# x[dst] stored turned: the first layer without its turn and its bias addition, and 391 gathers in place of 392

## The reference

```
row, col = src, dst                               # 50000 each, sorted by dst
h = (x @ W).reshape(N, 4, 32)
alpha = leaky_relu(s_src[row] + s_dst[col], 0.2)  # s_*: h times a vector, per head
ex = exp(alpha - m[row])                          # m: segment max over row, at least 0
alpha_n = ex / denom[row]
out = segment_sum(alpha_n * h[col], col) + bias
x = layernorm(x + out)
```

## Time and profile before

| what | us |
|---|---|
| median of 3 runs | 5133.67 |
| lowest and highest | 5132.33, 5134.39 |
| profiled execution | 5133.19 |
| its span | 5131.1 |

### The profile page before, as it was taken

The page is one execution under the profiler, slowest core; times in us unless marked ns, Lnnn a source line. Parts: engine busy times, 40 slices in busy tenths (PEclk is TensorE's granted clock), DMA queues, the critical chain, the costliest instruction groups (busy, mean ns, idle before and its releaser), DMA issues. The chain is left out here.

```text
span 5131.1 us, 72170 instructions
## 1 busy us (share of the span) xinstructions
PE 3158.9 (62%) x15758; PEld 2416.0 (47%) x15758; DVE 3395.8 (66%) x11785; ACT 2872.1 (56%) x7156; POOL 3650.5 (71%) x3635
## 2 busy tenths in 40 slices
PE   3555555545562666256477746666988787777774
PEld 3555455533441444145466644444555465555552
DVE  6587655658887777467399973333677776666664
ACT  0014666638874888268367762333455566666663
POOL 5777777767775777478677717776777677777777
PEclk9985555569986888689688878898556598888897
DMA  3336888868882777356478858887677632222222
GB/s 72 79 80 190 250 253 255 249 124 250 251 245 67 225 226 225 111 161 200 136 202 222 221 158 246 224 226 208 194 214 210 186 74 71 73 71 71 72 72 61
DMA packets 820081, 862.65 MB, mean 168 GB/s; under 512 B 161385, under 2 KB 595150, under 8 KB 819228
## 3 DMA queue, kind: packets, MB, share of 16 engines
q1 hardware_dynamic: 703656, 673.59, 43.0%
q0 software_dynamic: 112896, 179.36, 15.8%
q10 hardware_dynamic: 3314, 7.36, 0.4%
HBM read 494.63 MB, written 370.82 MB: 169 GB/s over the span
## 5 line engine op out<-in xcount | busy, mean ns | idle before, releaser
L1929 POOL DMA_INDIRECT gs_xs<-t_t,kept_idx_b x392 | 369.9, 944 | 229.7 <-issue 118.9
L1035 POOL DMA_INDIRECT t_alpha<-gsm_raw,gsm_edge_idx x392 | 386.1, 985 | 165.8 <-issue 116.7
L2193 POOL DMA_INDIRECT mss_xs<-t_x,kept_idx_a x392 | 387.2, 988 | 144.7 <-issue 118.2
L2185 POOL DMA_INDIRECT out_dram<-mss_o,kept_scat_idx x392 | 396.1, 1011 | 119.4 <-issue 118.2
L1227 PE MATMUL gsm_hp<-kept_w,gsm_zT 128*128 128x128 f32 x1568 | 253.9, 311 | 352.3 <-ACT gsm_zT L1093 351.9
L2049 POOL DMA_INDIRECT gs_xs<-t_z,kept_idx_a x392 | 369.9, 944 | 137.5 <-issue 119.2
L1598 POOL DMA_INDIRECT att_xs<-t_t,kept_idx_a x392 | 372.0, 949 | 134.2 <-issue 118.0
L1025 POOL DMA_INDIRECT gsm_raw<-t_al,kept_idx_b x392 | 378.4, 965 | 124.4 <-issue 118.6
L536 POOL DMA_INDIRECT sort_xs<-in_x_dram,kept_src_idx x392 | 379.5, 968 | 119.5 <-issue 119.5
L534 POOL DMA_INDIRECT sort_xd<-in_x_dram,kept_dst_idx x392 | 379.4, 968 | 119.4 <-issue 119.4
L216 PE MATMUL gs_tp<-kept_ident,gs_xs 128*128 128x128 f32 x784 | 268.9, 362 | 270.4 <-DMA gs_xs<-t_t,kept_idx_b 156.6
(11 more groups left out here) (556 smaller groups left out, 11023.8 us busy)
## 6 DMA issues: line engine op xcount, KB each, us to landing
t_t<-sort_o SPq DMA_DIRECT2D x61, 858.0 KB
t_x<-gsm_o SPq DMA_DIRECT2D x196, 264.0 KB
sort_x<-in_x_dram SPq DMA_DIRECT2D x61, 832.0 KB
gsm_x<-t_t SPq DMA_DIRECT2D x196, 256.0 KB
t_z<-gsm_z SPq DMA_DIRECT2D x196, 256.0 KB
out_dram<-gsm_o SPq DMA_DIRECT2D x196, 256.0 KB, 3.0
t_t<-l_o SPq DMA_DIRECT2D x49, 528.0 KB, 3.0
att_own<-t_t SPq DMA_DIRECT2D x98, 264.0 KB
```

The costliest lines, as they stand in the source:

```text
L1035: pool.indirect_dma_start(T["alpha"], bass.IndirectOffsetOnAxis(edge_idx[:, c:c + 1], 0), raw[:, c, :], None).then_inc(scattered[u], 16)
L1929: pool.indirect_dma_start(xs[u][:, j, :], None, T["t12"], bass.IndirectOffsetOnAxis(K["idx_b"][:, c:c + 1], 0)).then_inc(gathered[u], 16)
L2185: pool.indirect_dma_start(T["out"], bass.IndirectOffsetOnAxis(K["scat_idx"][:, c:c + 1], 0), o[q % BUFS][:, j, :], None, bounds_check=N - ...
L2193: pool.indirect_dma_start(xs[q % BUFS][:, j, :], None, T["x3"], bass.IndirectOffsetOnAxis(K["idx_a"][:, c:c + 1], 0)).then_inc(gathered[q ...
```

## The change

1. The sort stage stores `xdT`, which ACT has copied from PSUM, instead of the gathered rows: a table `xdstT` of 98 x 128 rows of 512 numbers (2 KB, as before). `xdT` has four buffers. The wait for this store moves from POOL's gather to ACT's copy, and SP's store moves from slot s to slot s+1.
2. The first layer loads the turned tiles into `xT` (four buffers), multiplies them at once, and turns them back: `accumulate_turned` puts x and the turned bias (made once, at the start) into one PSUM buffer `back`. ACT copies that to `x`, POOL adds once. ACT's order in a slot becomes root (item s-3), copy (s), apply (s-3); DVE's lags fall by two. SP's load waits for the multiply and the turn back of item s-4.
3. The 392nd chunk is left out of the gathers in five stages and of the last scatter, and the waits count 16 less for the last item. `gat_softmax` is as it was.

```diff
+FILLED = -(-E // P)
+def chunks_of(q):
+    return min(4 * q + 4, FILLED) - 4 * q
+def landed(t, u, each=16):
+    if is_item(t, u, ITEMS - 1):
+        return each * (4 * t + chunks_of(ITEMS - 1))
+    return 4 * each * t + 4 * each
+def turned_rows(table, t, u, width=4):
+    rows = table[bass.ds(t * (BUFS * P * width // 4) + u * (P * width // 4), P * width // 4), :]
+    return rows.rearrange("(k p) f -> p k f", p=P)
+def as_turned_rows(tile):
+    return tile.rearrange("p (k j) i -> p k (j i)", j=4)
...
# scores_and_sort
-        xdT = [sb(f"xdT{v}", [P, 4, P]) for v in range(2)]
+        xdT = [sb(f"xdT{u}", [P, 4, P]) for u in range(BUFS)]
...
-                wait_item(pool, xd_stored, t, u, 4, 16)
                 wait_item(pool, turned, t, u, 4)
-                for j in range(4):
+                for j in range(chunks_of(q)):
...
             def copy(t, u):
                 act.wait_ge(turned[u], t + 1)
                 wait_item(act, scored, t, u, 2)
-                act.copy(xdT[u % 2][:], tpd[u % 2][:]).then_inc(copied[u], 1)
+                wait_item(act, xd_stored, t, u, 4, 16)
+                act.copy(xdT[u][:], tpd[u % 2][:]).then_inc(copied[u], 1)
...
             def store_xd(t, u):
-                sp.wait_ge(gathered[u], 128 * t + 128)
-                sp.dma_start(tile_rows(T["xdst"], t, u), as_tile_rows(xd[u][:])).then_inc(xd_stored[u], 16)
+                sp.wait_ge(copied[u], 2 * t + 1)
+                sp.dma_start(turned_rows(T["xdstT"], t, u), as_turned_rows(xdT[u][:])).then_inc(xd_stored[u], 16)
...
-            parts = [(store_o, BEFORE + 2, WIDES), (load_x, BEFORE - 2, WIDES), (store_al, 3), (store_xd, 0)]
+            parts = [(store_o, BEFORE + 2, WIDES), (load_x, BEFORE - 2, WIDES), (store_al, 3), (store_xd, 1)]
...
# first_layer
             def load(t, u):
-                wait_item(sp, summed, t, u, 4)
-                sp.dma_start(as_tile_rows(x[u][:]), tile_rows(T["xdst"], t, u, G)).then_inc(loaded[u], 16)
+                wait_item(sp, multiplied, t, u, 4)
+                wait_item(sp, turned_back, t, u, 4)
+                sp.dma_start(as_turned_rows(xT[u][:]), turned_rows(T["xdstT"], t, u, G)).then_inc(loaded[u], 16)
...
-            def shift(t, u):
-                pool.wait_ge(turned[u], t + 1)
-                pool.tensor_tensor(x[u][:], x[u][:], K["bias0"][:].unsqueeze(1).broadcast_to([P, G, D]), ALU.add).then_inc(shifted[u], 1)
...
-            pipeline(pool, (add, 3, EIGHTS), (shift, 1, EIGHTS))
+            pipeline(pool, (add, 0, EIGHTS))
...
-            def turn(t, u):
+            def multiply(t, u):
                 pe.wait_ge(loaded[u], 16 * t + 16)
-                wait_item(pe, copied, t, u, 1)
-                for j in range(G):
-                    tr = pe.transpose(tp[:, j, :], x[u][:, j, :], K["ident"][:])
-                tr.then_inc(turned[u], 1)
-
-            def multiply(t, u):
-                pe.wait_ge(copied[u], t + 1)
                 wait_item(pe, scaled, t, u, 2)
                 for j in range(G):
-                    mm = pe.matmul(hp[u % 2][:, j, :], xT[u % 2][:, j, :], K["wh"][:], start=True, stop=True)
+                    mm = pe.matmul(hp[u % 2][:, j, :], xT[u][:, j, :], K["wh"][:], start=True, stop=True)
                 mm.then_inc(multiplied[u], 1)
-            pipeline(pe, (multiply, 1, EIGHTS), (turn, 0, EIGHTS))
+            def turn_back(t, u):
+                wait_item(pe, shifted, t, u, 1)
+                for j in range(G):
+                    tr = accumulate_turned(pe, back[:, j, :], xT[u][:, j, :], biasT[:], K["ident"])
+                tr.then_inc(turned_back[u], 1)
+            pe.transpose(back[:, 0, :], K["bias0"][:], K["ident"][:]).then_inc(bias_turned, 1)
+            pe.wait_ge(bias_copied, 1)
+            pipeline(pe, (multiply, 0, EIGHTS), (turn_back, 0, EIGHTS))
...
             def copy(t, u):
-                act.wait_ge(turned[u], t + 1)
-                wait_item(act, multiplied, t, u, 2)
-                act.copy(xT[u % 2][:], tp[:]).then_inc(copied[u], 1)
+                act.wait_ge(turned_back[u], t + 1)
+                wait_item(act, summed, t, u, 4)
+                act.copy(x[u][:], back[:]).then_inc(shifted[u], 1)
+            act.wait_ge(bias_turned, 1)
+            act.copy(biasT[:], back[:, 0, :]).then_inc(bias_copied, 1)
...
-            pipeline(act, (copy, 0, EIGHTS), (lambda t, u: norm_root(norm, act, t, u), 4, EIGHTS), (lambda t, u: norm_apply(norm, act, t, u, stored), 5, EIGHTS))
+            pipeline(act, (lambda t, u: norm_root(norm, act, t, u), 3, EIGHTS), (copy, 0, EIGHTS), (lambda t, u: norm_apply(norm, act, t, u, stored), 3, EIGHTS))
...
-            pipeline(dve, (measure, 4, EIGHTS), (scale, 2, EIGHTS), (lambda t, u: norm_scale(norm, dve, t, u), 4, EIGHTS))
+            pipeline(dve, (measure, 2, EIGHTS), (scale, 0, EIGHTS), (lambda t, u: norm_scale(norm, dve, t, u), 2, EIGHTS))
```

More of the change, by code:

```diff
@@ L751, in turn @@
             def turn(t, u):
-                pe.wait_ge(gathered[u], 128 * t + 128)
+                pe.wait_ge(gathered[u], landed(t, u, 32))
                 wait_item(pe, copied, t, u, 2, 2)
@@ L763, in score @@
                 for j in range(4):
-                    pe.matmul(sps[:, j, 0:HEADS], xdT[u % 2][:, j, :], K["wa"][:, HEADS:8], start=True, stop=False)
+                    pe.matmul(sps[:, j, 0:HEADS], xdT[u][:, j, :], K["wa"][:, HEADS:8], start=True, stop=False)
                     mm = pe.matmul(sps[:, j, 0:HEADS], xsT[u % 2][:, j, :], K["wa"][:, 0:HEADS], start=False, stop=True)
@@ L1377, in norm_of, with norm_measure @@
     return norm
-def norm_measure(norm, dve, t, u, added=None):
+def norm_measure(norm, dve, t, u, added=None, halves=None):
     for g in range(norm["width"]):
+        if halves is not None and g % 4 == 0:
+            dve.wait_ge(halves[u], 2 * t + g // 4 + 1)
         bn = dve.bn_stats(norm["stats"][u][:, g, :], norm["y"][u][:, g, :])
@@ L1440, in first_layer @@
         sb, ps, sem, sems, owned = stage_makers(nc, ctx, "l0")
+        xT = [sb(f"xT{u}", [P, G, P]) for u in range(BUFS)]
+        biasT = sb("biasT", [P, P])
         x = [sb(f"x{u}", [P, G, D]) for u in range(BUFS)]
-        xT = [sb(f"xT{v}", [P, G, P]) for v in range(2)]
         y = [sb(f"y{u}", [P, G, D]) for u in range(BUFS)]
         o = [sb(f"o{u}", [P, G, ROW1]) for u in range(BUFS)]
-        tp = ps("tp", [P, G, P])
+        back = ps("back", [P, G, P])
         hp = [ps(f"hp{v}", [P, G, D]) for v in range(2)]
-        loaded, turned, copied, multiplied = sems("loaded"), sems("turned"), sems("copied"), sems("multiplied")
-        shifted, scaled, summed, stored, o_set = sems("shifted"), sems("scaled"), sems("summed"), sems("stored"), sem("o_set")
+        loaded, turned_back, shifted, multiplied = sems("loaded"), sems("turned_back"), sems("shifted"), sems("multiplied")
+        scaled, summed, stored = sems("scaled"), sems("summed"), sems("stored")
+        bias_turned, bias_copied, o_set = sem("bias_turned"), sem("bias_copied"), sem("o_set")
         norm = norm_of(sb, sems, K["eps"], y, [tile[:, :, 0:D] for tile in o], width=G, ps=ps)
@@ L1959, in turn @@
             def turn(t, u):
-                pe.wait_ge(gathered[u], 64 * t + 64)
+                pe.wait_ge(gathered[u], landed(t, u))
                 pe.wait_ge(own_loaded[u], 16 * t + 16)
@@ L2197, in _ @@
             for u in range(BUFS):
-                pool.wait_ge(scattered[u], 64 * PER_BUF[u])
+                last = ITEMS - 1 - (ITEMS - 1 - u) % BUFS
+                pool.wait_ge(scattered[u], 64 * (last // BUFS) + 16 * chunks_of(last))
         @block.tensor
@@ L2266, in scale_x @@
             def scale_x(q):
-                act.wait_ge(gathered[q % BUFS], 64 * (q // BUFS) + 64)
+                act.wait_ge(gathered[q % BUFS], 64 * (q // BUFS) + 16 * chunks_of(q))
                 if q >= 2:
@@ L2403, in tables @@
     T["totals"] = dram("t_totals", (HEADS + 2, EP))
-    T["xdst"] = dram("t_xdst", (EP, D))
+    T["xdstT"] = dram("t_xdstT", (ITEMS * P, 4 * P))
     T["t12"] = dram("t_t12", (EP + N + EP, ROW1))
```

2 lines of the change are left out of this document (1 added, 1 removed).

## The result

The changed kernel takes 5072.39 us (median of 4, 5069.20 to 5074.13) against 5134.03 (median of 4) for the kernel before: ratio 0.9877, 95% interval 0.9865 to 0.9890. The profiled execution took 5074.13 us, its span is 5072.4 against 5131.1.

The account below looks back on a forecast made before the run. The prediction took a first-layer loop of load, copy, apply and store as the bound; 43 us from that layer plus 7.6 for the chunk made 51 off 5133.19, so 5082 us, range 5073 to 5104.

Parts of the forecast that it names:

- What bounds: First layer: a load, copy, apply, store loop gives 5.27 us a slot; once opened, ACT binds at 4.29.
- The first layer's size: First layer: last apply ends at 2427.4 instead of 2470.35, a gain of 43 us.
- 2223.8 + 191.4 + 12.2: First layer: fill end, 44 slots and three last slots, summed to the last apply's end at 2427.4.
- Fill: First-layer start: load wait 5 us, item 0 at 1.2 GHz, the next three 3.9 us each; second apply ends about 2223.8.
- Slots: First layer, slots 5 to 48: 44 slots at 4.35 us, ACT's 4.29 plus an allowance for clock dips.
- Tail: First-layer end: three slots without a copy at DVE's pace of 4.05 us, 12.2 us in all.
- The chunk: Leaving out the 392nd chunk in several stages saves 7.6 us in sum, bounds 3 and 9.
- Two gathers less in sort, 2 x 1.27: Sort stage end: PE waits for the last gathers, so two fewer save 2.5 us.
- Sort stage, the moved wait: Sort stage: moving the store wait from POOL's gather to ACT's copy costs nothing, bounds 0 and 5 us.
- PE through one PSUM buffer: First layer: short pauses might halve PE's clock, giving 7.1 us a slot and about 5213 us; chance 0.03.
- ACT and DVE do hook into each other: First-layer rival: slots of 4.5 to 4.9 us, 7 to 24 us more, 5089 to 5106; chance 0.20.
- The signs: ACT idle before copy under 10 us, POOL adds 4.3 to 4.4 apart, stage about 238, 1.3 us per gather.

Follow-up runs that it names:

- b1: Kernel before, with GpSimd's bias addition left out of the first layer (output lacks the bias): 5141.94 us against 5142.19, ratio 1.0002.
- b2: Kernel before, with only ACT's first-layer order changed to root, apply, copy: 5111.12 us against 5142.19, ratio 0.9940.
- a3: Changed kernel with ACT's copy ahead of its root in the first layer: 5108.89 us against 5143.25 for the kernel before, ratio 0.9936.
- c4: Changed kernel, first layer written out without hardware loop, one of eight applies on GpSimd ahead of its add: 5062.02 us, ratio 0.9858 to the kernel before.
- c3: Changed kernel with the first layer's pipelines written out on every engine, without the hardware loop: 5067.03 us against 5132.96 for the kernel before, ratio 0.9871.
- b4: Kernel before, with only the 392nd chunk left out: 5131.82 us against 5143.25, ratio 0.9980.
- a1: Changed kernel with the 392nd chunk gathered and scattered again: 5091.53 us against 5143.25 for the kernel before, ratio 0.9904.
- a0: Changed kernel timed again, unaltered: 5075.44 us against 5139.95 for the kernel before, ratio 0.9874.
- a2: Changed kernel with the old first-layer orders and lags of ACT and DVE: 5423.13 us against 5142.19 for the kernel before, ratio 1.0546.
- b3: Kernel before, with ACT's order root, apply, copy and without GpSimd's bias addition in the first layer: 5093.10 us against 5142.19, ratio 0.9907.
- c2: Changed kernel with one of eight first-layer applies on GpSimd, ahead of its add: 5073.95 us against 5137.10 for the kernel before, ratio 0.9877.
- b5: Kernel before, with the last chunk's indices taken from the chunk two places earlier, so its rows differ: 5144.09 us in one run.

## Why the prediction was right or wrong

- *What bounds.* Right. The loop through copy, apply, store and load was the limit (b1, b2); ACT is the limit after it, then DVE (a3, c4).
- *The first layer's size: wrong, 43 us forecast and 50.3 measured.* The step "2223.8 + 191.4 + 12.2" was too long in all three terms, by 3.3 + 3.5 + 0.6 us.
  - Fill, the largest miss against its size: the second apply ends 28.5 us after the first load's issue (2186.53 to 2215.07), 31.8 were taken. The load was there after 3.9 us and not 5.0 (3.7 to 3.9 in the kernels with the turned table, 4.4 to 5.3 in those without, which no run explains). The first item took PE 5.7 us and not 7.1, for the granted clock rose from 0.50 to 1.00 within its turn-back. The three after it took 3.53 each and not 3.9, in which the drain of the multiply was counted although the turn-back starts before its end.
  - Slots: 44 in 187.9 us (2215.07 to 2402.98), 4.27 each in place of 4.35. That this came so near is luck, for three errors met. ACT's 4.29 was 0.12 too long, since the eight applies were priced up to the end of the last, and the root starts 0.1 us ahead of that end. The dips of the clock, for which 0.06 was added, did not come. What makes 4.27 of ACT's 4.17 is the loop's jump (c3). The working had no term for it; the earlier trace rows do not show it, but the trace of before does.
  - Tail: three slots of 3.85 in place of 4.05.

  The range had bounds for the slot, but none for fill and tail.
- *The chunk: wrong in size.* 7.6 us forecast; b4 gives some 10 (its interval of 5 to 15 would still hold 7.6), and a1's gain of 51.7 is 10 to 13 under the changed kernel's in its two timings (61.6 and, as a0, 64.5). The stages decide it: "Two gathers less in sort, 2 x 1.27" counted only their issue, and the stage ends 5 us earlier. PE's wait of 6.11 us in the earlier trace rows could not tell when the last gather lands; the 4.09 us from the end of its issue to PE's turn could. The 1.27 us for `gcn_first` were short as well, 3.6 on the mean over the profiles; why, no run shows.
- *Sort stage, the moved wait: right.* The gap before the gathers (the page's line, to set beside the earlier trace rows) is what it was:

```profile
L557 POOL DMA_INDIRECT sort_xd<-in_x_dram,kept_dst_idx x391 | 379.4, 970 | 119.1 <-issue 119.1
```

  The stage is not longer for it (a1 ends at 1062.22 with the moved store, the kernel before at 1062.67).
- *PE through one PSUM buffer.* Right, and the granted clock is 1.00 from 2218 to 2400 us (before, 0.96 from 2218 to 2440), with PE busy 160 of the 182 us; it stands 0.4 us ahead of its multiply in most slots and 0.9 in the long ones. The rule of the Trainium skill on short PSUM pauses ("TensorE: Matmul & The Clock Gate", "A second HAM failure mode: psum-queue depth-cycling") is not borne out by this stage: the pauses are there, and the clock does not swing. a2, which is granted 0.71, pauses for 5.9 us at a time and says nothing on short pauses.
- *The rivals.* ACT and DVE do hook into each other, but only once in four slots, and for 0.5 us. (In the earlier trace rows the next statistics begin 0.31 us after 2221.91, not 0.37; nothing hangs on it.)
- *The signs.* PE's wait for the load after the fill is gone, as said. ACT's idle time ahead of the copy fell to 18.3 us and not under 10, because of the fill. GpSimd's adds are mostly 4.17 apart and not 4.3 to 4.4, the stage takes 232 us and not 238, and the end of sort moved by 2.6 us a gather and not 1.3.

## What to carry to other kernels

Before pricing an operation that is taken off an engine, find the loop that closes through the buffers and the order of each engine: the same GpSimd operation was worth 0 us in b1 and 17 us in b3, and one line of ACT's order 31. Price an engine that is full from start to start, not up to the end of its last instruction. Then price the fill and the tail with bounds as the slot has them, and the last transfer of a stage by when it lands, not by when it is issued. When two engines are within some tenths of a microsecond of each other, look for the slot that is longer than the others, at the jump of the hardware loop.

## What the runs showed of the hardware

- At the jump of its hardware loop DVE stood 0.30 to 0.34 us between two of its own instructions. Where it had 0.12 us a slot to spare beside ACT, one slot in four was 0.5 us longer, 0.12 us a slot on the mean over four. With the loops of all engines written out, the stage fell by 3.4 us (c3 to a0) and by 8.9 (c4 to c2).
- A last gather of 128 times the same row let PE go on 2.98 to 4.09 us after the end of its issue in five kernels, one of 128 different rows after 1.64 us in the one kernel that had it (b5). One with 48 equal rows of 128 took 3.26 (b4), so the cause is not settled.
- Eight applies took ACT 3.09 us from the first to the start of the next instruction in the changed kernel, where the last ends 0.1 us after that start; in b3, with the old table, 3.08. Both have slots of 4.17 us.
